# Marking tiles' places in the expert lists on ScalarE instead of VectorE, in most groups

## What is computed

```python
x = x + ga * _L0_attn_ref(h, ...)          # layer 0's mixer
h = _layernorm(x, axis=-1) * (1 + cb) + sb
x = x + gb * _L0_ffn_ref(h, ...)           # each token goes to its TOP TWO of 8 experts
...
x = x + ga * _L1_attn_ref(h, ...)          # layer 1's mixer
h = _layernorm(x, axis=-1) * (1 + cb) + sb
x = x + gb * _L1_ffn_ref(h, ...)           # each token goes to its best ONE of 8 experts
```

## Time and profile before

| | us |
|---|---|
| median of 3 runs | 1272.58 (1270.6 to 1275.98) |
| the profiled execution, its own time | 1274.55 |
| its span in the trace | 1272.7 |

### The profile page before, as it was taken

The page is one execution under the profiler, slowest core; times in us unless marked ns, Lnnn a source line. Parts: engine busy times, 40 slices in busy tenths (PEclk is TensorE's granted clock), DMA queues, the critical chain, the costliest instruction groups (busy, mean ns, idle before and its releaser), DMA issues. The chain is left out here.

```text
span 1272.7 us, 14828 instructions
## 1 busy us (share of the span) xinstructions
PE 897.0 (70%) x4200; PEld 569.9 (45%) x4200; DVE 919.8 (72%) x1848; ACT 590.5 (46%) x1298; POOL 767.3 (60%) x509
## 2 busy tenths in 40 slices
PE   3757877987898686762599915777786978338940
PEld 3413333433443232341599912345464756228940
DVE  6448799979988999969476744586795978464522
ACT  2264654576557646420144411546647585215620
POOL 0059679968997999830566558365534545236636
PEclk9878987997999898975699966889987968658975
DMA  6035344534643455421133411121101111142223
GB/s 173 1 104 173 120 133 149 165 115 130 179 154 125 139 164 171 138 97 44 32 86 87 81 50 44 48 57 34 44 10 42 43 50 34 34 167 59 66 58 99
DMA packets 85664, 117.72 MB, mean 92 GB/s; under 512 B 12688, under 2 KB 42576, under 8 KB 85456
## 3 DMA queue, kind: packets, MB, share of 16 engines
q1 hardware_dynamic: 78928, 103.13, 26.5%
q0 software_dynamic: 6656, 13.64, 4.9%
HBM read 102.52 MB, written 14.22 MB: 92 GB/s over the span
## 5 line engine op out<-in xcount | busy, mean ns | idle before, releaser
L484 PE MATMUL y_ps<-ma_h,ident 128*128 128x512 f32 x512 | 272.6, 668 | 75.4 <-POOL ma_h L711 43.6
L701 POOL TENSOR_TENSOR ma_bu<-ma_u,ma_row_b 128x1024 f32<-128x1024 f32 x128 | 298.6, 2357 | 16.8 <-DVE decay_ps L786 16.6
L605 ACT ACTIVATE decay_ps<-ma_delta,negA 128x512 f32<-128x512 f32 x256 | 173.0, 688 | 100.2 <-DVE ma_h L794 96.7
L1102 POOL DMA_INDIRECT s_rows<-xs,take x112 | 126.2, 1126 | 135.9 <-POOLq L867 78.1
L484 PEld LDWEIGHTS y_ps<-ma_h,ident 128*128 128x128 f32 x512 | 102.5, 212 | 228.1 <-issue 104.3
L786 DVE TENSOR_TENSOR_SCAN decay_ps<-decay_ps,ma_bu 128x512 f32<-128x512 f32 x96 | 115.7, 1220 | 32.1 <-ACT decay_ps L605 27.4
L1119 PE MATMUL s_up_ps<-s_xt,s_w 128*128 128x128 f32 x896 | 125.4, 286 | 7.8 <-issue 6.5
L794 DVE TENSOR_TENSOR ma_h<-decay_ps,ma_row_c 128x512 f32<-128x512 f32 x192 | 129.7, 676 | 0.0
L786 DVE TENSOR_TENSOR_SCAN decay_ps<-decay_ps,ma_carry,ma_bu 128x512 f32<-128x512 f32 x96 | 121.2, 1279 | 0.0
L1119 PEld LDWEIGHTS s_up_ps<-s_xt,s_w 128*128 128x128 f32 x896 | 115.8, 202 | 8.6 <-issue 6.8
L1128 PE MATMUL s_out_ps<-s_w,s_ht 128*128 128x128 f32 x608 | 89.6, 283 | 7.2 <-DVE s_outs L1195 7.0
(11 more groups left out here) (300 smaller groups left out, 1780.1 us busy)
## 6 DMA issues: line engine op xcount, KB each, us to landing
ma_row_b<-bc_rows SPq DMA_DIRECT2D x128, 256.0 KB, 3.6
ma_row_c<-bc_rows SPq DMA_DIRECT2D x128, 256.0 KB, 3.3
mi_cs<-cs_rows SPq DMA_DIRECT2D x32, 256.0 KB, 3.4
ys<-s_outs SPq DMA_DIRECT2D x28, 256.0 KB
w<-in_experts SPq DMA_DIRECT2D x1, 4112.0 KB, 13.4
w<-in_experts SPq DMA_DIRECT2D x1, 3072.0 KB, 10.7
xs<-rows SPq DMA_DIRECT2D x4, 512.0 KB, 3.7
out<-X SPq DMA_DIRECT2D x8, 256.0 KB
```

The lines of the kernel that those rows point to most:

```text
L484: mm = pe.matmul(y_ps[:, j, :], m.ident[:], h[g % HS][:, j, :], start=False, stop=True, skip_group_check=True)
L605: act.activation(decay[s % DS][:], delta[b % 2][:, j, col(c)], ACT.Exp, scale=m.negA0[:, j, n:n + 1]).then_inc(decay_done, 1)
L701: pool.tensor_tensor(bu[g % BUS][:], u[b % 2][:, :, col(c)], both(row_b[g % BS]), ALU.mult).then_inc(bu_done, 1)
L1102: pool.indirect_dma_start(rows[s % ROWS][:], None, m.xs[layer], bass.IndirectOffsetOnAxis(ap=m.take[:, s:s + 1], axis=0)).then_inc(fetched ...
```

## The change

ScalarE writes `at_spot` for some groups, and VectorE for the others; `in_slot` stays on VectorE everywhere. The groups of ScalarE are 1, 2, 4, 5 and 7 of the eight in layer 0, and 1 and 3 of the four in layer 1. For one tile ScalarE computes |column − spot| (Abs, with the negated `spot` as the bias column), eight instructions in a group, and then once for the group max(0, 1 − that) (Relu, scale −1, bias 1), which is one where the distance is zero and zero elsewhere. A new small VectorE instruction makes the negated spots (`spot_below`, 32-bit) and raises the new semaphore `split`, for which ScalarE waits. TensorE waits for `marked` (two counts in such a group, not three) and in ScalarE's groups also for `spot_step`. Three pairs of semaphores of the last norm are merged into `moment_step` and `root_step`, with the same order of waits.

```diff
+    groups = choices * TILES // MARK
+    by_act = [g for g in range(groups) if (g % 3 > 0 if layer == 0 else g % 2 == 1)]
+    own_marks = lambda g: sum(2 if q in by_act else 3 for q in range(g))
...
+        spot_below = sb("spot_below", [P, choices, TILES])
...
@@ tensor
-                        pe.wait_ge(marked, marks + 3 * ((k * TILES + t) // MARK) + 3)
+                        g = (k * TILES + t) // MARK
+                        pe.wait_ge(marked, marks + own_marks(g + 1))
+                        if g in by_act:
+                            pe.wait_ge(spot_step, act_marks + 2 * by_act.index(g) + 2)
...
@@ scalar
-                act.wait_ge(var_done, 1)
-                act.activation(var[:], var[:], ACT.Ln).then_inc(var_log, 1)
-                act.wait_ge(var_log, 1)
-                act.activation(var[:], var[:], ACT.Exp, scale=-0.5).then_inc(rstd_done, 1)
-                act.wait_ge(shift_done, 1)
+                act.wait_ge(moment_step, 1)
+                act.activation(var[:], var[:], ACT.Ln).then_inc(root_step, 1)
+                act.wait_ge(root_step, 1)
+                act.activation(var[:], var[:], ACT.Exp, scale=-0.5).then_inc(root_step, 1)
+                act.wait_ge(moment_step, 2)
...
+            act.wait_ge(split, done)
+            for i, g in enumerate(by_act):
+                k, t0 = divmod(g * MARK, TILES)
+                for t in range(t0, t0 + MARK):
+                    near = act.activation(at_spot[:, k, t, :], m.counth[:], ACT.Abs, bias=spot_below[:, k, t:t + 1])
+                near.then_inc(spot_step, 1)
+                act.wait_ge(spot_step, act_marks + 2 * i + 1)
+                group = at_spot[:, k, t0:t0 + MARK, :]
+                act.activation(group, group, ACT.Relu, scale=-1.0, bias=1.0).then_inc(spot_step, 1)
...
@@ vector
             step_of(dve.tensor_copy(spot[:], parts[:, 1]))
+            dve.tensor_scalar(spot_below[:], parts[:, 1], -1.0, None, ALU.mult).then_inc(split, 1)
...
-                    dve.tensor_tensor(at_spot[:, k, T, :], m.counth[:].unsqueeze(1).broadcast_to(A),
-                                      spot[:, k, T].unsqueeze(2).broadcast_to(A), ALU.is_equal).then_inc(marked, 1)
+                    if of not in by_act:
+                        dve.tensor_tensor(at_spot[:, k, T, :], m.counth[:].unsqueeze(1).broadcast_to(A),
+                                          spot[:, k, T].unsqueeze(2).broadcast_to(A), ALU.is_equal).then_inc(marked, 1)
```

More of the change, by code:

```diff
@@ L314, in make_norm @@
     return norm
-ROUTE_SEMS = "step chosen_done counted marked taken"
+ROUTE_SEMS = "step chosen_done counted marked taken split spot_step"
 def mamba(nc, m):
@@ L888, in route @@
         spot = sb("spot", [P, choices, TILES], F16)
+        spot_below = sb("spot_below", [P, choices, TILES])
         at_spot = sb("at_spot", [P, choices, TILES, P], F16)
         in_slot = sb("in_slot", [P, choices, TILES, slots], F16)
-        step, chosen_done, counted, marked, taken = (m.sems["ro_" + n] for n in ROUTE_SEMS.split())
-        done, marks = layer + 1, 3 * layer * CHOICES[0] * TILES // MARK
+        step, chosen_done, counted, marked, taken, split, spot_step = (
+            m.sems["ro_" + n] for n in ROUTE_SEMS.split())
+        done, marks, act_marks = layer + 1, *m.marks_before
+        m.marks_before = (marks + own_marks(groups), act_marks + 2 * len(by_act))
         if layer == 0:
@@ L898, in route @@
             lg_ps = ctx.enter_context(nc.psum_tensor(tag + "lg_ps", [P, BT * NE], F32))
-            var_done, var_log, rstd_done, shift_done, hat_done, act_hat_done, turned, written, lg_done, modulated = (
-                sem(n) for n in "var_done var_log rstd_done shift_done hat_done act_hat_done turned written lg_done "
-                "modulated".split())
+            moment_step, root_step, hat_done, act_hat_done, turned, written, lg_done, modulated = (
+                sem(n) for n in "moment_step root_step hat_done act_hat_done turned written lg_done modulated".split())
         block = ctx.enter_context(nc.Block())
@@ L972, in norm_last @@
                 settle()
-                dve.scalar_tensor_tensor(var[:], var[:], 1.0 / P, tmp[:], ALU.mult, ALU.add).then_inc(var_done, 1)
-                dve.wait_ge(rstd_done, 1)
-                dve.scalar_tensor_tensor(tmp[:], mean[:], -1.0, var[:], ALU.mult, ALU.mult).then_inc(shift_done, 1)
+                dve.scalar_tensor_tensor(var[:], var[:], 1.0 / P, tmp[:], ALU.mult, ALU.add).then_inc(moment_step, 1)
+                dve.wait_ge(root_step, 2)
+                dve.scalar_tensor_tensor(tmp[:], mean[:], -1.0, var[:], ALU.mult, ALU.mult).then_inc(moment_step, 1)
                 for t in range(HALF, BT):
@@ L1033, in _ @@
                     T = slice(g * MARK, (g + 1) * MARK)
-                    before = marks + 3 * (k * (TILES // MARK) + g)
+                    of = k * (TILES // MARK) + g
+                    before = marks + own_marks(of)
                     A, B = [P, MARK, P], [P, MARK, slots]
@@ L2042, in build @@
         m.route_steps = [0]
+        m.marks_before = (0, 0)
         setup(nc, a, m)
```

## The result

The changed kernel took 1270.44 us (median of 15 runs, 1266.05 to 1275.12), the kernel before 1275.98 us (15 runs, 1270.6 to 1279.06): a ratio of 0.9958, 95% interval 0.9943 to 0.9973. The three runs on which the prediction rested lay at the low side of the fifteen, so the ratio is the number to hold against the forecast of 0.9961.

What follows compares the result with a forecast made beforehand. The prediction took VectorE's building of the lists as the bound, with ScalarE the bound after the change; gains of 3.50 us in layer 0 and 1.49 in layer 1 gave 1272.58 − 5.0 = 1267.6 us, range 1262.5 to 1272.5.

Steps and rivals of the forecast that it cites:

- What bounds the lists: Both list-building stretches: VectorE busy throughout (19.78 and 7.76 us); each microsecond by which take comes earlier shortens the whole time.
- VectorE's terms: VectorE's list work after the change: owners' chain ends at 603.98 in layer 0, 1129.74 in layer 1; alone, gain 6.82 us.
- The group without a mark: VectorE in a layer 0 group whose at_spot ScalarE writes: 1.47 us, against 2.47 with the mark.
- ScalarE's terms: ScalarE's group: eight Abs 2.47 us at L1669's price, 0.03 wait, Relu 0.95 to the next start, together 3.45 us.
- Who is last: End of both stretches: ScalarE becomes the bound, take at 605.39 against VectorE's 603.98, in layer 1 1130.16 against 1129.74.
- The sum: Gain of both layers' stretches together: 3.50 + 1.49 = 4.99 us.
- The dear ScalarE: Rival on ScalarE's list work: 16-bit activations priced nearer L941, gain between −0.2 and 3 us, about 1271.1; chance 0.12.
- the disturbed loops: Rival: ScalarE's 63 added instructions make the expert loops stumble at their start, one more 6.2 us stall, 1273.8; chance 0.10.
- the barrier held by the weights: Rival in layer 1: the weights' landing holds the block's barrier, so layer 1 gives nothing, 1269.1; chance 0.05.
- the prediction's own sign: Stated sign of being wrong: both stretches shrink as said and the expert loops behind them grow.
- the VectorE bound: Rival: ScalarE cheap, VectorE sets the lists' end, gain 6.8 us to 1265.7 or lower; chance 0.18 for over 6.4.
- The base: Starting time of the kernel before, from three runs' median: 1272.58 us, with a median's error of 1 to 2 us.

Runs made afterwards that it cites:

- e4_four: Changed kernel with four of layer 0's eight groups (1, 3, 5, 7) on ScalarE, not five; ratio to the kernel before 0.9950, timed again 0.9955.
- e5_all: Changed kernel with all groups' at_spot marks on ScalarE, eight in layer 0 and four in layer 1; ratio to the kernel before 1.0087.
- e6_spare: Changed kernel with ScalarE's 63 activations written to a spare tile nobody reads, VectorE writing all marks; ratio to the kernel before 1.0009.
- e3_layer1: Changed kernel with ScalarE's groups in layer 1 alone, none in layer 0; ratio to the kernel before 0.9989.
- e1_none: Changed kernel with no groups on ScalarE, VectorE writing all marks, the other edits kept; ratio to the kernel before 1.0007.
- e7_scalar: Changed kernel with no marks on ScalarE and VectorE's marks made per tile by narrow scalar-column instructions; ratio to the kernel before 1.0052.
- e9_gpsimd: Changed kernel with in_slot's multiplication on GpSimd, ScalarE's groups 1, 3, 5 in layer 0 and 1 in layer 1; ratio to the kernel before 0.9989.

## Why the prediction was right

*What bounds the lists.* Right. VectorE filled both stretches before, and time taken from them came off the whole: ten different kernels, from −5.5 to +12.1 us in the stretches, follow in their measured ratios within 0.0011, inside every interval. Anything else between the stretches and the total is below 1.4 us, which is what 0.0011 of the time comes to.

*VectorE's terms.* The group without a mark: 1.46 us against 1.47. One small step was wrong: the added instruction was charged 0.11 us on VectorE. From L1029 to L1036 it was 0.22 us, and from L1046 to L1055, with the new instruction between, it is 586.43 − 586.21 = 0.22 us. It runs in a gap in which VectorE waited for its own copy anyway. Since ScalarE sets the end, the step touches no part of the sum.

*ScalarE's terms.* Eight Abs in 2.44 us against 2.47, a group in 3.44 against 3.45, the Relu in 1.057 against 1.05. The choice of L1669 over L941 and L1158 decided the sum: at L941's price nothing would have been left. The 16-bit form costs what the 32-bit one does, 386 against 390 ns. The Trainium skill ("ScalarE: Activation LUTs", What ACT_TABLE_LOAD costs) states one element a cycle for 32-bit floats and bfloat16; these runs add the 16-bit float of this kernel.

*Who is last.* ScalarE, as forecast: by 1.50 us in layer 0 (1.41 forecast; VectorE idle for 1.54), and in layer 1 by 1122.63 − (1120.65 + 1.43) = 0.55 us (0.42 forecast; idle for 0.59). e4_four and e5_all confirm it from both sides.

*The sum.* 3.50 + 1.49 = 4.99 us forecast, 3.55 + 1.47 = 5.02 us in the stretches, 5.4 us (0.42% of 1275.98) in the runs. Part of the closeness is luck, as small errors cancel. In layer 0 ScalarE starts 0.32 us behind the copy's start (0.36 forecast) and its list takes 603.76 − 586.53 = 17.23 us (17.35), while the product and the handovers behind it take 604.65 − 603.76 = 0.89 us (0.78).

*The rivals.* The dear ScalarE, the disturbed loops and the barrier held by the weights are each shown not to happen (the form's row, e6_spare, e3_layer1). The two loops are 1.2 us longer in the changed kernel's profile than in that of before; by the prediction's own sign that would count against it, but e1_none, without ScalarE's marks, has the same 1.2 us, and e6_spare, with all of ScalarE's instructions, is 0.8 us shorter than before, so ScalarE's work does not make it. Of the VectorE bound, e4_four reaches 5.51 us; the 6.82 us of the prediction would need five groups at the price of L1158, which reads PSUM; the 16-bit form from SBUF does not have it ((2.44 − 0.386)/7 = 0.293 us apart, against 0.257).

*The base.* The absolute 1267.6 us is 2.8 us under the measured 1270.44, all of it because the first three runs of before lay 3.4 us under the median of fifteen. The prediction had allowed 1 to 2 us for that, which was too little.

## What to carry to other kernels

An engine that fills a serial stretch while another is idle is worth splitting. Here each layer's gain was priced to 0.05 us before the run, from rows that matched in each operand's kind (its memory, its scalar columns); the first guesses for e7_scalar and e9_gpsimd, priced from rows that did not match or as if the engines did not meet, missed by 13 and 9 us. The split is best where both engines end together, and the last consumer's own tail counts: here 0.89 us of product and handovers stood behind ScalarE's last instruction while VectorE's share hid under its own chain. GpSimd is no free third hand beside VectorE when both read two operands from SBUF.

## What was unexpected of the hardware

- VectorE and GpSimd take turns: with GpSimd multiplying beside it, VectorE's 128x576 went from 0.76 to 1.22 us and its 128x1024 from 1.22 to 1.78 us in the mean. GpSimd's own instruction of 576 16-bit elements spans 1.9 us in the mean, but that holds its waiting: behind the end of VectorE's instruction it needs about 1.0 us, an estimate from 604.49 − 603.48, where 1.3 had been estimated from its 128x1024 rows. ScalarE beside both kept its price: eight Abs in 2.43 or 2.44 us.
- A VectorE instruction with 32-bit scalar columns on short 16-bit rows takes 0.16 us (one column, 128 elements) to 0.21 us (two columns, 72 elements; 0.20 with 40) from start to start, against 0.11 us for a small instruction without a column.
- A VectorE instruction placed where the engine waits for its own last result cost nothing (0.22 us with it and without).
